# Local attention on one core: the last steps of its last layer in a written-out order

## What is computed

```python
def local_attention(q, k, v):
...
    sim = jnp.einsum('bhwie,bhwje->bhwij', bq, bk2) * QK_SCALE
    sim = jnp.where(mask, -jnp.finfo(sim.dtype).max, sim)
    attn = jax.nn.softmax(sim, -1)
    out = jnp.einsum('bhwij,bhwje->bhwie', attn, bv2)
...
def ffn_layer(x, g, bln, W1, b1, W2, b2):
    mu = x.mean(-1, keepdims=True)
    var = ((x - mu) ** 2).mean(-1, keepdims=True)
    xn = (x - mu) / jnp.sqrt(var + 1e-05) * g + bln
    hg = xn @ W1 + b1
    a, gate = jnp.split(hg, 2, -1)
    return a * jax.nn.gelu(gate, approximate=False) @ W2 + b2
```

## Time and profile before

| what | value |
|---|---|
| median of 3 executions | 4086.07 us (4070.82 to 4088.09) |
| the profiled execution, own time | 4077.11 us |
| its span in the trace | 4075.3 us |
| mean granted clock of TensorE | 0.95 |
| step 17 of the last layer starts (scores of block 15) | 1804.20 us of the span |
| last addition to the residual stream ends | 1868.84 us |
| first matmul of stage 1 | 1869.71 us |
| instructions | 121721 |

### The profile page before, as it was taken

How to read it: one execution, slowest core, us unless ns; L and a number is a source line. 1 busy time by engine, 2 the same in 40 slices (tenths; PEclk the granted TensorE clock), 3 DMA queues, 4 the chain that set the end, 5 groups by cost and what they waited for, 6 DMA issues and landing times.

```text
span 4075.3 us, 121721 instructions
## 1 busy us (share of the span) xinstructions
PE 3685.5 (90%) x50424; PEld 2022.6 (50%) x50424; DVE 3047.6 (75%) x5108; ACT 2540.2 (62%) x3819; POOL 1249.2 (31%) x1096
## 2 busy tenths in 40 slices
PE   6789999999999999988998999999988699999998
PEld 2355555555555555554644555555554233333333
DVE  7788988888888989864637666767676777777772
ACT  6456666766666666655436555556564476767775
POOL 0465656656666656640100000000002011112221
PEclk8899999999999999986589999999999799999999
DMA  2122222223222222221000000000001211111100
GB/s 73 34 66 78 70 70 76 73 61 81 75 65 79 71 77 70 70 54 26 22 1 3 4 4 5 4 4 2 4 7 41 93 21 21 21 21 21 26 2 11
DMA packets 84728, 163.77 MB, mean 40 GB/s; under 512 B 26648, under 2 KB 36552, under 8 KB 82912
## 3 DMA queue, kind: packets, MB, share of 16 engines
q1 hardware_dynamic: 83937, 155.06, 14.6%
q10 hardware_dynamic: 223, 0.61, 0.1%
HBM read 40.88 MB, written 8.52 MB: 12 GB/s over the span
## 4 chain that ended last, share of the span: by engine, by line
PE 38%; issue 23%; POOL 19%; DVE 11%; ACT 6%; DMA 0%; POOLq 0%; SPq 0%; DVEq 0%; ACTq 0%
POOL arena L1428 9%; POOL arena L1432 8%; PE banks L1768 6%; PE banks L3067 5%; PE banks L1731 3%; ACT arena L3212 2%; PE banks L1749 2%; DVE arena L1938 2%; PE banks L3025 2%; PE banks L3041 2%; PE banks L1787 2%; POOL arena L1412 2%; DVE arena L1957 1%; DVE arena L3295 1%; DVE arena L1311 1%
## 5 line engine op out<-in xcount | busy, mean ns | idle before, releaser
L3295 DVE TENSOR_REDUCE arena<-banks 128x2 f32<-128x1024 f32 x512 | 613.6, 1222 | 199.9 <-PE banks L3032 94.8
L3212 ACT ACTIVATE arena<-banks 128x1024 f32<-128x1024 f32 x512 | 521.3, 1025 | 217.3 <-PE banks L3048 104.3
L1428 POOL TENSOR_TENSOR arena<-arena 128x512 f32<-128x512 f32 x384 | 425.2, 1129 | 630.5 <-DVE arena L1311 622.9
L1432 POOL TENSOR_TENSOR arena<-arena 128x1024 f32<-128x1024 f32 x192 | 533.0, 2776 | 15.1
L1938 DVE CUSTOM_DVE_ANT_0 arena<-arena,banks 128x512 f32<-128x512 f32 (+3 forms) x640 | 361.7, 602 | 143.7 <-issue 138.6
L960 PE MATMUL banks<-arena 128*128 128x512 f32 x768 | 368.9, 625 | 27.2 <-issue 14.6
L1876 ACT ACTIVATE arena<-banks 128x512 f32<-128x512 f32 (+3 forms) x320 | 168.9, 528 | 336.0 <-PE banks L1750 334.9
L3067 PE MATMUL banks<-arena 128*32 128x256 f32 x4096 | 334.8, 394 | 13.0 <-issue 7.9
L1868 ACT ACTIVATE arena<-arena 128x128 f32<-128x128 f32 (+15 forms) x256 | 328.7, 1285 | 14.3 <-DVE arena L1950 9.7
L1731 PE MATMUL banks<-arena 64*128 64x512 f32 (+3 forms) x1280 | 318.1, 572 | 6.9 <-issue 4.8
L2020 POOL COPY arena<-arena 128x512 f32<-128x512 f32 x32 | 19.8, 617 | 991.9 <-DVE arena L1964 991.9
(11 more groups left out here) (448 smaller groups left out, 7571.5 us busy)
## 6 DMA issues: line engine op xcount, KB each, us to landing
arena<-arena SPq DMA_DIRECT2D x768, 64.0 KB, 2.4
arena<-arena SPq DMA_DIRECT2D x96, 384.0 KB, 3.6
arena<-arena SPq DMA_DIRECT2D x104, 128.0 KB, 3.4
arena<-in_lf_wqkv SPq DMA_DIRECT2D x6, 1024.0 KB, 5.4
arena<-arena SPq DMA_DIRECT2D x8, 512.0 KB
arena<-features_k SPq DMA_DIRECT2D x30, 128.0 KB
arena<-features_q SPq DMA_DIRECT2D x15, 216.0 KB
arena<-in_lf_wqkv SPq DMA_DIRECT2D x6, 512.0 KB, 4.3
```

Source lines behind the costliest of these rows:

```text
L1428: nc.gpsimd.tensor_tensor(r[:, :, e * H2:(e + 1) * H2], q[:, j, :, (1 - e) * H2:(2 - e) * H2], s[:, j, 1, e * H2:(e + 1) * H2].unsqueeze(1 ...
L1432: nc.gpsimd.tensor_tensor(a, a, lf_rb, ALU.add).then_inc(S("lf_rot" + x), 1)
L3212: nc.scalar.activation(bi_PT[n % 4], PS[:, 2 * bi_slot("S", n):2 * bi_slot("S", n) + 2].rearrange("p a b -> p (a b)"), ACT.Exp).then_inc(S ...
L3295: nc.vector.tensor_reduce(bi_max[j % 2][:, t, :, c], PS[:, 2 * slot:2 * slot + 2], AX.X, ALU.max).then_inc(S("bi_mx"), 1)
```

## The change

`lf_steps` takes a `tail`; with it the last layer's steps end at step 16, and the tail is issued in place of steps 17 to 24 on TensorE, ScalarE and VectorE. SyncE and GpSimd keep their steps. The last block's transposition no longer waits for the values of block 14; SyncE waits for them ahead of that block's eight transfers. `lf_pair` gives the pair of banks of an `up`. `project`, `values`, `scores`, the norm's pieces and `affine` are unchanged but for a bank. Where `end` is true the Gelu table is loaded for m=0 only, and the Ln and Exp table is loaded once, behind `keep_o(15)`. The three `tail` functions in the diff are those of TensorE, ScalarE and VectorE, in this order.

```diff
         def lf_steps(eng, step, tail=None):
...
-            for s in range(LEAD, NB + 9):
+            for s in range(LEAD, NB + 1 if tail else NB + 9):
                 step(DEPTH - 1, s, True)
+            if tail:
+                tail(DEPTH - 1)
+
+        def lf_pair(c, m, end):
+            if end and c == 2:
+                return (2, 3) if m == 1 else (6, 7)
+            if end and c == 3:
+                return ((6, 7), (0, 1), (2, 3))[m]
+            return 6, 7
...
             def pair_windows(n, l, end):
                 sp.wait_ge(S("lf_pt"), l * NB + (n + 1))
+                if end and n == NB - 1:
+                    sp.wait_ge(S("lf_pv"), l * NB + n)
...
-                    dve.wait_ge(S("lf_pv"), l * NB + n)
+                if n >= 1 and not (end and n == NB - 1):
+                    dve.wait_ge(S("lf_pv"), l * NB + n)
                 nc.vector.transpose(lf_PT.rearrange("p a b -> p (a b)"), lf_E2.rearrange("p a b -> p (a b)")).then_inc(S("lf_pt"), 1)
...
-            def gate(c, m, l):
-                nc.scalar.preload_act_table_set(GELU_SET)
+            def gate(c, m, l, end=False):
+                if not end or m == 0:
+                    nc.scalar.preload_act_table_set(GELU_SET)
...
+            def down_part(m, l):
+                pe.wait_ge(S("lf_h"), l * 12 + (10 + m))
+                k = FT[m][1]
+                mm = nc.tensor.matmul(PS[:, 5], lf_w2[0:k, m], lf_G[m][0:k], start=(m == 0), stop=(m == 2), skip_group_check=True)
+                if m == 2:
+                    mm.then_inc(S("lf_o"), 1)
...
+            def both(c, m, l):
+                for j in range(2):
+                    up(c, m, l, j, True)
+
+            def tail(l):
+                scores(NB - 1, l, True, 0)
+                scores(NB - 1, l, True, 1)
+                ffn_taken(NB, l, True)
+                both(2, 0, l)
+                project(NB - 3, l, True)
+                values_ready(NB - 2, l, True)
+                values(NB - 2, l, 0)
+                values(NB - 2, l, 1)
+                both(2, 1, l)
+                project(NB - 2, l, True)
+                pe.wait_ge(S("lf_h"), l * 12 + 7)
+                both(2, 2, l)
+                values_ready(NB - 1, l, True)
+                values(NB - 1, l, 0)
+                values(NB - 1, l, 1)
+                project(NB - 1, l, True)
+                pe.wait_ge(S("lf_h"), l * 12 + 8)
+                mean(3, l, 2)
+                down(2, l, 3)
+                var(3, l)
+                both(3, 0, l)
+                both(3, 1, l)
+                down_part(0, l)
+                pe.wait_ge(S("lf_y"), l * NCH + (NCH + 3))
+                both(3, 2, l)
+                down_part(1, l)
+                down_part(2, l)
...
+            def tail(l):
+                affine(2, l)
+                exps(NB - 1, l)
+                gate(2, 0, l, True)
+                keep_o(NB - 2, l)
+                gate(2, 1, l, True)
+                gate(2, 2, l, True)
+                keep_o(NB - 1, l)
+                nc.scalar.preload_act_table_set(LN_EXP_SET)
+                shifted(3, l)
+                square(3, l)
+                deviation(3, l)
+                affine(3, l)
+                for m in range(3):
+                    gate(3, m, l, True)
...
-            for c in range(NCH):
+            def residual(c):
                 dve.wait_ge(S("lf_y"), DEPTH * NCH + c + 1)
                 nc.vector.tensor_tensor(ck(xT, c), ck(xT, c), ck(lf_y[:, 1:T + 1], c), ALU.add).then_inc(S("x_ffn0"), 1)
+
+            def tail(l):
+                normed(2, l)
+                soft(NB - 1, l)
+                inverse(NB - 1, l)
+                probs(NB - 1, l, True)
+                add(NB - 3, l)
+                product(2, 0, l, True)
+                residual(0)
+                residual(1)
+                add(NB - 2, l)
+                product(2, 1, l, True)
+                product(2, 2, l, True)
+                add(NB - 1, l)
+                centre(3, l, 2)
+                out_(2, l, 3)
+                normed(3, l)
+                residual(2)
+                product(3, 0, l, True)
+                product(3, 1, l, True)
+                product(3, 2, l, True)
+                out_(3, l, 5)
+                residual(3)
```

More of the change, by code:

```diff
@@ L235, in program, with lf_steps @@
         RL2 = 20
-        def lf_steps(eng, step):
+        def lf_steps(eng, step, tail=None):
             for s in range(LEAD):
@@ L304, in shift_v, with pair_windows @@
                 sp.dma_start(vs[0:WIN], lf_V[(n - 1) % 4][P - WIN:P]).then_inc(S(f"lf_vs{n % 2}"), 16)
-            def pair_windows(n, l):
+            def pair_windows(n, l, end):
                 sp.wait_ge(S("lf_pt"), l * NB + (n + 1))
+                if end and n == NB - 1:
+                    sp.wait_ge(S("lf_pv"), l * NB + n)
                 for a in range(4):
@@ L340, in step @@
                 if lf_live(s - 2, end):
-                    pair_windows(s - 2, l)
+                    pair_windows(s - 2, l, end)
                 if more and s == NB + 3:
@@ L1064, in project, with mean @@
                 m.then_inc(S("lf_wo"), 1)
-            def mean(c, l):
+            def mean(c, l, bank=6):
                 pe.wait_ge(S("lf_xs"), l * 8 + (2 * c + 2))
-                nc.tensor.matmul(PS[:, 6], avg, lf_xc, start=True, stop=True).then_inc(S("lf_mean"), 1)
+                nc.tensor.matmul(PS[:, bank], avg, lf_xc, start=True, stop=True).then_inc(S("lf_mean"), 1)
             def var(c, l):
@@ L1073, in var, with up @@
                 nc.tensor.matmul(PS[:, 4], avg, lf_sx, start=True, stop=True).then_inc(S("lf_var"), 1)
-            def up(c, m, l, j):
+            def up(c, m, l, j, end=False):
                 if m == 0 and j == 0:
@@ L1082, in up, with down @@
                 f = f0 + FF * (1 - j)
-                nc.tensor.matmul(PS[0:k, 6 + j], lf_w1[:, f:f + k], lf_xc, start=True, stop=True).then_inc(S("lf_amm" if j else "lf_gmm"), 1)
-            def down(c, l):
+                nc.tensor.matmul(PS[0:k, lf_pair(c, m, end)[j]], lf_w1[:, f:f + k], lf_xc, start=True, stop=True).then_inc(S("lf_amm" if j else "lf_gmm"), 1)
+            def down(c, l, bank=7):
                 pe.wait_ge(S("lf_h"), l * 12 + (3 * c + 3))
@@ L1090, in down @@
                     k = FT[m][1]
-                    mm = nc.tensor.matmul(PS[:, 7], lf_w2[0:k, m], lf_G[m][0:k], start=(m == 0), stop=(m == 2))
+                    mm = nc.tensor.matmul(PS[:, bank], lf_w2[0:k, m], lf_G[m][0:k], start=(m == 0), stop=(m == 2))
                 mm.then_inc(S("lf_o"), 1)
+            def down_part(m, l):
[4 more added lines that the diff above has]
+                    mm.then_inc(S("lf_o"), 1)
             def step(l, s, end):
@@ L1131, in step @@
                     values(s - 3, l, 1)
-            lf_steps(pe, step)
+            def both(c, m, l):
[29 more added lines that the diff above has]
+                down_part(2, l)
+            lf_steps(pe, step, tail)
         def lf_act(act):
@@ L1231, in gate @@
                 act.wait_ge(S("lf_gmm"), l * 12 + (3 * c + m + 1))
-                nc.scalar.activation(lf_G[m][0:k], PS[0:k, 6], ACT.Gelu, bias=lf_vec[0:k, 5 + m:6 + m]).then_inc(S("lf_gelu"), 1)
+                nc.scalar.activation(lf_G[m][0:k], PS[0:k, lf_pair(c, m, end)[0]], ACT.Gelu, bias=lf_vec[0:k, 5 + m:6 + m]).then_inc(S("lf_gelu"), 1)
             def step(l, s, end):
@@ L1266, in lf_act @@
                 block_in(n, 0)
-            lf_steps(act, step)
+            def tail(l):
[13 more added lines that the diff above has]
+                    gate(3, m, l, True)
+            lf_steps(act, step, tail)
         def lf_dve(dve):
@@ L1325, in inverse, with probs @@
                 nc.vector.reciprocal(lf_st[:, 1], lf_st[:, 1]).then_inc(S("lf_rsum"), 1)
-            def probs(n, l):
+            def probs(n, l, end):
                 dve.wait_ge(S("lf_rsum"), l * NB + (n + 1))
@@ L1341, in add, with centre @@
                 nc.vector.tensor_tensor(lf_y2[:, 1 + t * P:1 + (t + 1) * P], lf_y[:, 1 + t * P:1 + (t + 1) * P], PS[:, 5, 0:P], ALU.add).then_inc(S("lf_y2"), 1)
-            def centre(c, l):
+            def centre(c, l, bank=6):
                 dve.wait_ge(S("lf_mean"), l * NCH + (c + 1))
-                nc.vector.tensor_tensor(lf_xc, lf_xc, PS[:, 6], ALU.subtract).then_inc(S("lf_xc"), 1)
+                nc.vector.tensor_tensor(lf_xc, lf_xc, PS[:, bank], ALU.subtract).then_inc(S("lf_xc"), 1)
             def normed(c, l):
@@ L1349, in normed, with product @@
                 nc.vector.tensor_tensor(lf_xc, lf_xc, lf_sx, ALU.mult).then_inc(S("lf_xhat"), 1)
-            def product(c, m, l):
+            def product(c, m, l, end=False):
                 k = FT[m][1]
@@ L1356, in product, with out_ @@
                 dve.wait_ge(S("lf_amm"), l * 12 + (3 * c + m + 1))
-                nc.vector.scalar_tensor_tensor(out=lf_G[m][0:k], in0=PS[0:k, 7], scalar=lf_vec[0:k, 2 + m:3 + m], in1=lf_G[m][0:k],
```

(13 more changed lines are left out.)

## The result

| | before | after |
|---|---|---|
| median of 4 executions | 4083.53 us (4070.82 to 4088.09) | 4060.85 us (4056.37 to 4064.39) |
| profiled execution, own time | 4077.11 us | 4064.39 us |
| its span | 4075.3 us | 4062.2 us |
| stretch from the scores of block 15 to the last addition | 1804.20 to 1868.84, 64.6 us | 1814.25 to 1856.39, 42.1 us |
| from there to the end of the span | 2206.5 us | 2205.8 us |

What follows compares the result with a forecast made beforehand. The prediction saw one long dependence in the 65 us stretch, with no engine full. Terms of 6.8 + 4.7 + 3.2 - 1.3 + 6.8 + 1.9 gave 22.1, discounted to 20.3: 4086.07 - 20.3 = 4065.8 us, range 4051 to 4080.

Steps and rivals of the forecast that it cites:

- 1 landing of the last probabilities: Last block's eight transfers: they land 6.8 us earlier, since block 14's values no longer stand behind a product and a projection.
- 2 landing to end of values: After the last landing TensorE does only both halves of the values, 2.4 us instead of 7.1: 4.7 us gained.
- 3 to the mean's end: Last values to mean: chunk 2's Gelus and products are done ahead, 5.8 us instead of 9.0: 3.2 us gained.
- 4 mean to variance: Chunk 2's down projection now stands between mean and variance on TensorE: 1.3 us lost, 4 at the low clock.
- 5 chunk 3: Last chunk: nine products run in a row on three pairs of banks, 10.1 us instead of 16.85: 6.8 us gained.
- 6 additions: End of the stretch: three of four residual additions move to where VectorE waits: 1.9 us gained.
- Counting one pair of this as chance: Profiled execution's unlucky clock in the stretch: 1.8 us taken off, so the gain over a usual execution is 20.3.
- The other loads leave no trace of their own: ScalarE's dropped table loads: each lay beside a product's matmuls or was in another term already, so no separate gain.
- a clock that stays low: Rival: pauses in the new tail keep TensorE's clock low; gain only 3.3 to 12 us, 4078 in the middle; chance 0.13.
- tied pairs: Rival: chunk 3's pairs still wait for the VectorE product before, so its gain stays 0: 4072.6 us; chance 0.05.
- The early transposition: Last block's transposition no longer waits: at full clock it brings only 0.9 of the 6.8 us earlier landing.
- a fall of the clock in later stages: Rival: a later stretch falls to half clock, 177.5 us of it costing 88.8, giving 4154.6; chance of slower 0.04.

Runs made afterwards that it cites:

- t1: d3 with the old order's two table loads put back between the Gelus of chunk 3, four in all; stretch 42.9 us, 2.2 more than d3.
- b1: The kernel before the change with three products that nobody reads in each of three TensorE pauses (the filled old order); stretch 55.2 us.
- u3: Changed kernel with the three tiles of chunk 3 sharing one pair of banks (6 and 7) again; stretch 43.6 us against 42.1.
- d3: Changed kernel with products that nobody reads filling TensorE's four pauses; stretch 40.6 us, no low clock.
- u1: Changed kernel with the last transposition waiting for the values of block 14 again; stretch 47.9 us, 17.1 of it at low clock.
- u4: Changed kernel with the four additions to the residual stream at the end again; stretch 50.4 us, 25.6 of it at low clock.
- t2: d3 with the last transposition waiting for the values of block 14 again; stretch 41.5 us, no low clock.
- d4: Changed kernel with chunk 2's down projection cut into TensorE's pauses and the two remaining pauses filled; 4056.11 us, 0.9931 of before, stretch 39.8 us.
- after_again: The changed kernel measured once more, without edits; 4057.23 us, 0.9946 of before, stretch 40.7 us, no low clock.

## Why the prediction was right

The forecast was 4065.8 against a measured 4060.85, within the range, and step by step, in the stretch:

| step | forecast | measured |
|---|---|---|
| 1 landing of the last probabilities | 6.8 | 22.89 - 16.11 = 6.78 |
| 2 landing to end of values | 4.7 | 7.09 - 2.24 = 4.85 |
| 3 to the mean's end | 3.2 | 8.97 - 6.06 = 2.91 |
| 4 mean to variance | -1.3 | 1.43 - 2.57 = -1.14 |
| variance to first product | 0 | 4.23 - 3.88 = 0.35 |
| 5 chunk 3 | 6.8 | 16.85 - 9.78 = 7.07 |
| 6 additions | 1.9 | 3.18 - 1.50 = 1.68 |
| sum | 22.1 | 22.50 |

Before this comes from the earlier trace rows and after from the chain above. Of the new item of 0.35, 0.26 is the variance's own matmuls, which take 0.88 behind the down projection and 1.14 behind a pause. Each sign that the prediction named for the changed profile is there except two positions: the last transfers landed at 1830.37 and not near 1820.5, and stage 1's first matmul came at 1857.26 and not near 1848. Both are past the bounds that the prediction set for being wrong (1822 and 1855), because it gave them from the start of the span and the whole stretch began 10 us later; counted from the stretch's start they are as forecast.

How close the numbers are is partly luck. The interval of the ratio, 0.993 to 0.996, is a gain of 16 to 29 us, so it can't tell the forecast's 20.3 from the 22.5 of the stretch. And the 6.8 of step 5 took the middle between two states of the clock, which the first profile came near to (9.78 us for a forecast of 10.1); in the changed kernel's second profile, at the full clock, chunk 3 took 8.3, and the step would have been 8.5.

Four steps were wrong, or right in size and not in what they said of the cause:

- *"Counting one pair of this as chance, the gain over a usual execution is 20.3."* The undiscounted 22.1 fits the 22.7 of the medians better. The filled old order shows 9.4 us of low clock cost in the profiled execution before, whose three falls (1810.4, 1820.7 and 1848.0) each began in a pause of TensorE. How much of it other executions paid was not measured, as only one profile of before with its pauses exists. This discount put the forecast on the bound of 0.5%; the measured 0.55% has an interval on both sides of it, so no verdict between faster and unchanged by that bound is certain.
- *"The other loads leave no trace of their own."* True of the profile read, where pairs came every 4.7 us at the low clock. With the clock held, they space the Gelus: t1 lost 2.2 us by four of them. Had the clock been full before, step 5 would have had to carry them.
- *"24 of 65 us were low."* The third fall stands in the same rows, 6.7 us from 1810.5, and the record of the granted clock has 31.1 us in all. The prediction used these 6.7 us as another argument for that rival and left them out of the count; the chance of 0.13 for it rests on the smaller number.
- Step 5 as a whole (7.1) is little of what its name says. At the full clock the start of the first product to the start of the last `out_` takes 12.3 us in the old order (b1), 9.8 with one pair of banks (u3, less the 1.4 that its first pair lost to the clock) and 8.35 with three (d3). So banks bring 1.5, and the down projection in parts and single loads together 2.5. Of these 2.5 the parts are 1.8: from the last product on VectorE to `out_` it takes 3.75 us in b1 and 1.97 in u3. The remaining 3.1 of the step are the clock, 4.6 lost before less 1.5 after.

The rival of a clock that stays low did not decide here, but it is real: u1 and u4 fell into it in the middle of the stretch and lost some 5 us or more by it. The Trainium skill (TensorE: Matmul & The Clock Gate, A second HAM failure mode) tells of a kernel that cycles through banks, pauses between its groups and swings between the clocks. The cycling itself did no harm here: with three pairs of banks (the changed kernel) and with one (u3) the low clock was the same 3.4 us, and it was the single pair that had the pauses. By these two profiles the rise of the clock from 0.76 to 0.96 came with the rest of the order and not with the banks. The rival of tied pairs is refuted by the chain. The early transposition was rightly priced at 0.9 (t2: 0.90, u1: 0.72). For a fall of the clock in later stages there is no sign: from the stretch's end to the span's it took 2200.2 to 2209.5 us in all fourteen profiles.

## What to carry to other kernels

In a tail where nothing is full, write down what each transfer waits for and move every piece of TensorE's work that does not need it to the other side: here the work ahead of the last chunk was worth 9.0 us at the full clock, the parts of a sum 1.8 and more banks 1.5. Price pauses twice, once as time and once as the clock that they may lose, and compare such edits with the pauses filled, or one execution's clock passes for the effect. And an operation that lies beside slow matmuls is free only for as long as they are slow.

## What the runs showed of the hardware

- The same instructions ran into the low clock or did not: the changed kernel's stretch had 3.4 us and 0 us at 0.50 in its two profiles. Two variants (u1, u4) had 13.7 us in one piece behind a pause of 2.5 and 2.0 us ahead of the last values. From the values of block 14 to the last down projection the clock was 1.00 in all five kernels with filled pauses (d3, d4, b1, t1, t2), and in one of the nine profiles without (after_again). In d4 and t1 3.4 us ahead of these values were low, which cost nothing visible.
- A load of an activation table took 1.28 us, and where nothing else was awaited the next instruction began within 0.02 us of its end.
- One of the eight transfers that SyncE issues for block 14, the fifth, took 0.99 to 1.60 us on its queue in all fourteen profiles, the others 0.55 to 0.60, and so did all eight of the last block. What holds it up is not shown.
- The stretch began between 1802.0 and 1815.9 us, though what precedes it is the same code in all. Behind the stretch the spread was 9.3 us. Together they are more than most of the differences between the variants, which is why the stretch and not the time is compared. The low clock ahead of the stretch came to 71.7 to 95.6 us, least in the two that began first (u3, d1); whether that is the cause is not shown.
